# Masked attention layers: score products in fp32 on row strips, masks single-buffered; eight-bit feed-forward in stages

## What is computed

```python
x = x + attn(layernorm(x), ctx, ctx, mask...)     # layers 0, 1, 3
  q = (xn @ wq + bq), k = (ctx @ wk + bk), v = (ctx @ wv + bv)    # 16 heads of 16
  scores = q @ k.T / 4 (+ adj, layer 1);  masked -> NEG
  out = softmax(scores) @ v @ wo + bo
x = x + ffn_fp8(layernorm(x))                     # layer 2
  x_q = (bf16(xn) / s_in).astype(float8_e4m3fn);  k_q = (kernel / s_k).astype(float8_e4m3fn)
  y = bf16((x_q @ k_q) * (s_in * s_k)) + bias
```

## Time and profile before

| | us |
|---|---|
| median of three runs | 4533.09 |
| the profiled execution: its time / its span | 4538.09 / 4536.3 |
| TensorE / VectorE / ScalarE / GpSimd busy | 3469.7 / 2668.9 / 1727.2 / 1143.6 |
| mean granted TensorE clock | 0.868 of 2.4 GHz |
| attention 0 / 1 / 3 (stretches of the span) | 772 / 929 / 768 |
| fp8 feed-forward | 129 |
| bytes moved by DMA | 430 MB |

### The profile page before, as it was taken

How to read it: one execution, slowest core, us unless ns; L and a number is a source line. 1 busy time by engine, 2 the same in 40 slices (tenths; PEclk the granted TensorE clock), 3 DMA queues, 4 the chain that set the end, 5 groups by cost and what they waited for, 6 DMA issues and landing times. The chain is left out here.

```text
span 4536.3 us, 66863 instructions
## 1 busy us (share of the span) xinstructions
PE 3469.7 (76%) x17919; PEld 1709.7 (38%) x18053; DVE 2668.9 (59%) x7644; ACT 1727.2 (38%) x2466; POOL 1143.6 (25%) x1198
## 2 busy tenths in 40 slices
PE   2999998896477777867967777777325989997697
PEld 0343343443122222225634444444212334335465
DVE  1666665775488888974215555556664656663531
ACT  0454544442143344442115545555212545552011
POOL 3533430000643344201112222221004211201122
PEclk7999999898688888888988888888657999996699
DMA  5553550002544344310048888888224344323133
GB/s 123 96 101 67 99 90 16 5 1 58 109 110 85 85 85 89 67 44 0 0 82 238 225 223 229 224 234 239 68 50 64 55 69 67 55 36 103 34 97 74
DMA packets 198806, 430.47 MB, mean 95 GB/s; under 512 B 25392, under 2 KB 77456, under 8 KB 193696
## 3 DMA queue, kind: packets, MB, share of 16 engines
q1 hardware_dynamic: 192288, 417.74, 39.6%
q0 software_dynamic: 6144, 8.39, 1.1%
HBM read 265.38 MB, written 134.22 MB: 88 GB/s over the span
## 5 line engine op out<-in xcount | busy, mean ns | idle before, releaser
L420 DVE CUSTOM_DVE_ANT_0 A_sums<-A_p_ps,A_bias 128x512 bf16<-128x512 f32 x1536 | 1005.7, 686 | 560.7 <-PE A_p_ps L267 534.9
L493 ACT ACTIVATE A_probs<-A_p_ps 128x1024 f32<-128x1024 f32 x512 | 522.8, 1023 | 548.6 <-PE A_p_ps L285 546.9
L267 PE MATMUL A_p_ps<-A_k_stack,A_q_stack 96*128 96x512 bf16 x1536 | 537.8, 401 | 199.1 <-DVE A_nmax L420 191.1
L281 PE MATMUL A_p_ps<-A_q_stack,A_k_stack 99*128 99x512 bf16 x1536 | 477.3, 393 | 5.6 <-issue 2.4
L295 PE MATMUL A_oT_ps<-A_probs,A_v_aug 128*17 128x512 f32 x3072 | 435.2, 639 | 6.3 <-ACT A_probs L493 4.4
L493 ACT ACTIVATE A_probs<-A_probs 128x1024 f32<-128x1024 f32 x256 | 270.6, 1057 | 429.0 <-DVE A_probs L435 428.6
L267 PEld LDWEIGHTS A_p_ps<-A_k_stack,A_q_stack 96*128 96x128 bf16 x1536 | 138.9, 99 | 621.9 <-DVE A_nmax L420 529.1
L1070 DVE CUSTOM_DVE_ANT_0 A_scores<-A_qk_ps,A_rel_in 128x384 f32<-128x384 f32 (+3 forms) x512 | 232.1, 486 | 203.2 <-PE A_qk_ps L955 122.7
L978 PE MATMUL A_t_ps<-ident,A_scores 128*128 128x128 f32 x1280 | 226.2, 316 | 139.2 <-DVE A_probsT L1060 127.9
L435 DVE TENSOR_TENSOR A_probs<-A_p_ps,A_biasT 128x1024 f32<-128x1024 f32 x256 | 311.4, 1218 | 3.8 <-PE A_p_ps L281 3.4
L285 PE MATMUL A_p_ps<-A_biasT,ident_bf 128*128 128x512 bf16 x906 | 281.2, 380 | 7.2 <-issue 0.7
(11 more groups left out here) (341 smaller groups left out, 5407.4 us busy)
## 6 DMA issues: line engine op xcount, KB each, us to landing
A_parts_dram<-A_parts SPq DMA_DIRECT2D x48, 768.0 KB, 4.2
A_k_stack<-A_parts_dram SPq DMA_DIRECT2D x144, 256.0 KB, 9.8
A_q_stack<-A_parts_dram SPq DMA_DIRECT2D x144, 256.0 KB, 9.5
A_rel_dram<-A_rel_out SPq DMA_DIRECT2D x64, 512.0 KB, 4.4
A_rel_in<-A_rel_dram SPq DMA_DIRECT2D x64, 512.0 KB
A_rel_dram<-A_rel_out SPq DMA_DIRECT2D x64, 384.0 KB, 3.4
A_rel_in<-A_rel_dram SPq DMA_DIRECT2D x64, 384.0 KB, 4.1
A_ctxT<-in_ctxT SPq DMA_DIRECT2D x32, 512.0 KB, 12.4
```

The costliest lines, as they stand in the source:

```text
L267: nc.tensor.matmul(p1_ps[i % 2][:, :], q_stack[0:KS, a_par, j * GH + i, t * P:(t + 1) * P], k_stack[0:KS, a_par, j * GH + i, :], start=Tru ...
L281: last = nc.tensor.matmul(p2_ps[half][:, i % 2, :], k_stack[:, par, j * GH + i, kb * P:(kb + 1) * P], q_stack[:, par, j * GH + i, :], star ...
L420: nc.vector.tensor_tensor_reduce(out=sums[:, i % NX, :], in0=p1_ps[i % 2][:, :], in1=bias[:, (par + over) % NB, t, :], scale=-1.0, scalar= ...
L493: nc.scalar.activation(dst, src, ACT.Exp).then_inc(exp_done, 1)
```

## The change

In the three masked layers:

- q and k are stored once, in fp32, without parts: `q_stack` and `k_stack` become `[P, 2, NG, S]`, where head i of a group has rows 32i to 32i+15 (and 32i+16 is the row of maxima, against a row of ones in `k_stack`). Each product takes one strip of 32 rows. Splits, `parts_dram` and its stores go; a stack is loaded by 4 DMAs from `qk32` in SBUF (before: 1 store and 6 loads through DRAM). Maxima are turned in fp32 and placed by one DMA (before: 4).
- a position issues pass 1 and pass 2 by turns, on strips 0, 2, 1, 3 (p even) or 2, 0, 3, 1 (p odd), after all its waits.
- pass 1 and pass 2 each have a ring of three banks. ScalarE takes one head at a time (128x512).
- in layer 1 VectorE adds the bias to every other head (`LATE`); for the others TensorE adds it as three bf16 parts (`highT`, `midT`, `lowT`), three identity products.
- masks have one buffer, converted one block at a time, late in the frame; the hardware loop is written out; xT moves to 12 and 15, k to 18 and 20, and the first frame starts at p = 7.

`ffn_fp8`: ScalarE normalises, scales, multiplies for the overflow and copies the turned rows; VectorE keeps statistics, four of the rounding passes, the last add and the residual (one 128x1024 tile); buffers are doubled or tripled and the batches are staggered by one to three turns.

```diff
+    RW = P // GH
+    RING = 3
+    PAIRS = ((2, 3), (0, 1))
+    LOADS = GH
-        q_stack = sb("q_stack", [KS + 3, 2, H, S], BF16)
-        k_stack = sb("k_stack", [KS + 3, 2, H, S], BF16)
+        q_stack, k_stack = sb("q_stack", [P, 2, NG, S], F32), sb("k_stack", [P, 2, NG, S], F32)
-        p1_ps = [pb(f"p1_ps{i}", [P, S], F32) for i in range(2)]
-        p2_ps = [pb(f"p2_ps{i}", [P, 2, S], F32) for i in range(2)]
+        p1_ps = [pb(f"p1_ps{i}", [P, S], F32) for i in range(RING)]
+        p2_ps = [pb(f"p2_ps{i}", [P, S], F32) for i in range(RING)]
-        BY_DVE = (0, 1) if adj is not None else ()
+        LATE = (0, 2) if adj is not None else ()
+        TURNED_PARTS = (biasT,) if adj is None else (highT, midT, lowT)
-        FRONT = [(17, "k", 0), (20, "k", 1), (23, "xT", 0), (24, "xT", 1), (25, "q", 0), (28, "q", 1)]
+        FRONT = [(12, "xT", 0), (15, "xT", 1), (18, "k", 0), (20, "k", 1), (25, "q", 0), (28, "q", 1)]
-        START = 16
+        START = 7
+        def scores_read(n):
+            return (biased, adds(n + 1)) if by_dve(n) else (exp_done, n + 1)
...
+                    if later(unit + 2 - RING):
+                        pe.wait_ge(maxed, unit + 2 - RING)
+                    for k in (n, n + 1):
+                        if k >= RING:
+                            pe.wait_ge(*scores_read(k - RING))
+                for k in range(2):
+                    if first:
+                        i = 2 * half + k
+                        rows = slice(RW * i, RW * i + HD)
+                        nc.tensor.matmul(p1_ps[(unit + k) % RING][:, :], q_stack[rows, a_par, j, t * P:(t + 1) * P],
+                                         k_stack[rows, a_par, j, :], start=True, stop=True).then_inc(p1_done, 1)
+                    if second:
+                        i = PAIRS[half][k]
+                        rows = slice(RW * i, RW * i + HD + 1)
+                        last = nc.tensor.matmul(p2_ps[(n + k) % RING][:, :], k_stack[rows, par, g, kb * P:(kb + 1) * P],
+                                                q_stack[rows, par, g, :], start=True, stop=by_dve(n + k))
+                for k in range(2):
+                    if second and not by_dve(n + k):
+                        for part in TURNED_PARTS:
+                            last = nc.tensor.matmul(p2_ps[(n + k) % RING][:, :], ident_bf[:, :], part[:, kb, :],
+                                                    start=False, stop=part is TURNED_PARTS[-1])
+                        last.then_inc(p2_done, 1)
...
+            for i in range(GH):
+                sp.dma_start(stack[RW * i:RW * i + HD, par, :, :],
+                             qk32[i // 2:P:2, which, i % 2, :]).then_inc(stack_ready[which], 16)
...
@@ ffn_fp8
+            for n in range(B + 3):
+                if n + 1 < B:
+                    if n:
+                        statistics(n + 1)
+                    aggregate(n + 1)
+                if 0 <= n - 2 < B:
+                    finish_rows(n - 2)
+                if 0 <= n - 1 < B:
+                    round_rows(n - 1)
+                if 0 <= n - 3 < B:
+                    residual(n - 3)
...
+            for n in range(B + 2):
+                if n < B:
+                    normalise(n)
+                if n >= 2:
+                    turned(n - 2)
+                if 1 <= n <= B:
+                    overflow(n - 1)
+                if n >= 2:
+                    scaled_back(n - 2)
```

More of the change, by code:

```diff
@@ L188, in has @@
         def has(b, s):
[L190 removed]
+            return 0 <= b * STEPS + s < B * STEPS
         def ahead(s):
@@ L201, in group_split, with adds, by_dve @@
             return j if has(b, j * TPB) else None
-        def adds(step):
-            return step * len(BY_DVE)
+        def adds(n):
+            return n // GH * len(LATE) + sum(place < n % GH for place in LATE)
+        def by_dve(n):
+            return n % GH in LATE
+        def scores_read(n):
+            return (biased, adds(n + 1)) if by_dve(n) else (exp_done, n + 1)
         def pe_shared(pe, n, kind, i, base, b, par):
@@ new lines, in masked_attention, with mask_steps, pool_mask @@
+        MASK_STEPS = (lambda k: 1 + (k >= TPB)) if adj is not None else (lambda k: 0)
+        def mask_steps(bn, k):
+            return bn * sum(MASK_STEPS(i) for i in range(MK)) + sum(MASK_STEPS(i) for i in range(k))
+        def pool_mask(pool, bn, k):
+            done = (bn - 1) * STEPS + (NG - 1) * TPB + k % TPB + 1
+            if k < TPB and later(bn):
+                pool.wait_ge(maxed, done * GH)
+            if k >= TPB and later(bn):
+                pool.wait_ge(p2_done, done * GH)
+                if LATE:
+                    pool.wait_ge(biased, adds(done * GH))
+            dst = (bias if k < TPB else biasT)[:, k % TPB, :]
+            pool.wait_ge(mask_here[k % 2], (bn * (MK // 2) + k // 2 + 1) * MASK_LOADS)
@@ new lines, in pool_frame @@
+        def pool_frame(pool, b, par):
+            after, then = has(b, 0) and has(b + 1, 0), has(b + 2, 0)
+            for s in range(STEPS):
+                if s == 0 and every_mask and has(b, 0) and later(b):
+                    pool_mask(pool, b, MK - 1)
+                if s == 3 and has(b + 1, 0):
+                    pool_residual(pool, b + 1)
+                if s == 4 and then:
+                    pool_norm(pool, b + 2)
+                if s in (6, 7, 8, 9) and after and every_mask:
+                    pool_mask(pool, b + 1, s - 6)
+                if s in (13, 14, 15) and after and every_mask:
+                    pool_mask(pool, b + 1, TPB + s - 13)
@@ new lines, in overflow, with turned @@
+            def overflow(b):
+                act.wait_ge(rounded, b + 1)
+                if b >= 2:
+                    act.wait_ge(xq_ready, b - 1)
+                nc.scalar.activation(over[:, b % 2, :], v[:, b % 3, :], ACT.Copy, scale=FP8_PASS).then_inc(over_ready, 1)
+            def turned(b):
+                act.wait_ge(xqT_done, b + 1)
+                if b >= 2:
+                    act.wait_ge(y_done, (b - 1) * 2)
+                nc.scalar.activation(xqT[:, b % 2, :, :], t_ps[b % 2][:, :, :], ACT.Copy).then_inc(xqT_ready, 1)
```

621 lines of the change are left out of this document (268 added, 353 removed).

## The result

The changed kernel takes 4684.68 us (median of four runs, 4674.0 to 4690.51), the kernel before in the same rounds 4534.59 (4532.85 to 4550.21): a ratio of 1.032, 95% interval 1.0291 to 1.035. It is slower, by 150 us; 4662 was forecast. The profiled execution took 4686.68 us (span 4684.9), where the sum of the prediction came to 4667. One of the four executions of experiment 1 took 5313.95 us, at a mean granted clock of 0.63, and is left out of that experiment's median and ratio.

The account below looks back on a forecast made before the run. TensorE bounds layers 0 and 3, its loop with VectorE layer 1, VectorE the fp8 stage. On 4538.1 us: +70, +71, +30, -42 (layers 0, 3, 1, fp8) give 4667, median 4662; own range 4590 to 4760, full range 4450 to 4880.

Parts of the forecast that it names:

- (a): Score products, layers 0 and 3: four fp32 row strips run at once, 0.86 us a half, no change; upper bound 3.44.
- Partial overlap: Rival: strips overlap in part, 0.09 us paid for each of four strips, 207 us more, 4870 us; chance 0.16.
- no overlap: Rival: strips run one after another, 2.58 us a half, 1980 us more, 6640 us; chance 0.06.
- The rival of the clock: Rival: granted clock of layers 0 and 3 falls from 1.00 to 0.87, 175 us more, 4840 us; chance 0.04.
- (b): TensorE, layers 0 and 3: three more mode changes and unhidden first weights of two strip groups, 0.5 us a step, 8 a batch.
- The rival of free switches: Rival: strips next to full products cost nothing, 192 us less in the three masked layers, 4470 us; chance 0.27.
- (c): Ring of three banks, layers 0 and 3: uncovered even halves stall 0.73 us for exp, 5.4 us a batch.
- (d): Maxima, layers 0 and 3: m as four fp32 products costs 2.2 us a batch; 3 of 5.5 us of waits go.
- The last batch: Layers 0 and 3: half the halves lack pass 1, which saved 0.43 us each; strips last as long for two products, +6.
- Setup: Start of masked layers: first product at about 63 us, first frame 12 us longer; -30 layer 0, -29 layer 3, -15 layer 1.
- Layer 1: Loop between TensorE and VectorE of 2.75 us a half, plus about 5 us of delayed adds; batch 109 against 103, +45.
- fp8: Feed-forward stage: VectorE loses 48 us of work and waits, filling and draining the pipeline gives back 6; -42 us.

Follow-up runs that it names:

- experiment 1: The kernel before with only the new fp8 feed-forward, masked layers as they were; 4493.6 us, ratio 0.9895.
- experiment 5: The changed kernel with every group of four strips of layer 0 issued twice, the second overwriting the first with the same values; 4954 us.
- experiment 4: The changed kernel without mask products in layer 0 and with all score products of layer 3 reading the first strip of rows; 6053 us.
- Experiment 8: The changed kernel with one semaphore increment per group of value products instead of four, and in layer 0 one per two pass-1 products; 4668.77 us, ratio 1.0297.
- experiment 2: The changed kernel with four pieces of TensorE's shared work moved from odd halves to bare even halves; 4604.15 us, ratio 1.0142.
- experiment 3: The changed kernel, maxima over every fourth column in layers 0 and 3, two pass-1 and four pass-2 banks in layer 0; batches 90.0 us (layer 0), 93.8 (layer 3).
- experiment 6: The changed kernel with two banks for pass 1 and four for pass 2 in layer 0, maxima whole; 4720.9 us.
- experiment 7: The changed kernel with unused strips filled by products nobody reads, in the last batch of layers 0 and 3 and layer 0's first frame; 4650.74 us, ratio 1.0249.

## Why the prediction came out

**(a) The strips run at once: right.** Starts within 0.02 us, 0.86 us for a group without edges, 3.44 on one strip. Partial overlap and no overlap both fall. The rival of the clock falls for steady batches, which kept 1.00. The Trainium skill, "TensorE: Matmul & The Clock Gate", section "Measured speedup vs the span model", has 3.07 times for four row strips of 512 columns. Here a lone group of four fp32 products takes 1.07 us against 3.44, 3.2 times, and one that follows another 0.86, 4.0 times (experiment 5).

**(b) The switches: right, in both terms.** Three more changes at 0.11 us and 0.10 for each of the two strip groups make 0.53 us more for each step, where the prediction had 3 x 0.11 + 2 x 0.08 = 0.5. The rival of free switches falls with it. The Trainium skill, "TensorEngine Tiling (Array Packing)", section Tiling Modes, says that a change of mode drains the engine; the last pass ahead of each change is in fact 0.10 to 0.12 us longer, while two groups of one mode follow each other without a gap (experiment 5). The 0.10 at the start of a strip group is something else, since it is there without a change of mode too (experiment 4). That it is the load of the first weights, as the prediction says, is argued and not shown; the load (0.18 us) does begin together with the product, both at 546.58 in experiment 4. Experiment 8 excludes the increments.

**(c) The ring: right in mechanism and size.** 0.69 against 0.73 in bare even halves, 0.25 against 0.29 with a short turn, so 4.95 us a batch against 5.4; experiments 2, 3 and 6 show it from three sides. What was said to be queued behind the wait (pass 1 too) is what makes it dear.

**(d) The maxima: right, but the rest of VectorE's waits went too.** m costs 3.45 - 2.59 = 0.86 us a half (0.84 forecast). I kept 2.5 of the 5.5 us of waits for maxima in each batch; with three banks for pass 1, 0.2 us is left. Together with the 0.5 of the ring that is more than the 1.9 by which a batch came out lower than forecast (93.8 against 95.6; seven grew by 10.7 each, not 12.6). About 1 us goes the other way: a projection behind value products costs 1.92 us, not the 1.72 that I took.

**The last batch: the step that failed.** I gave it +12 us in all, and it took +36 in layer 0 and +32 in layer 3. Pass 1's absence saved 0.43 us a half before and saves nothing now, as I had written; but the clock, which I had priced only for the steady batches, falls there. Filled, and so at 1.00 to the end, the last batch takes 95.8 us: that is 12 us less in layer 3 and 16 in layer 0 (there in part the spread of executions), and still 20 more than before instead of 12. Waits for exp are 3 us of that (experiment 7's trace behind 804 us); the rest wasn't taken apart.

**Setup: nearly right.** The first product of pass 1 comes at 61.8 us (63 forecast). The first frame lasts 49 us where 42 was forecast, at a clock of 0.50 to 0.69. I had named the cold clock "at times"; it stayed for the whole frame, and the frame took 19 us more instead of 12. In layer 1 the first product came 24 us sooner and the first frame got 15 us longer: 9 us gained where 15 were forecast.

**Layer 1: one term too many.** The loop is as forecast: even halves 2.69 to 2.75 us (2.75), odd ones 2.81 (2.8). I added 5 us a batch for heads, norm and residual delaying an add; the sum without them is 103.9 us, and that is what a batch takes, not 109. One even half a batch lasts 3.40 us instead of 2.72; no more shows. The layer came out 12 us under the forecast, by this and in spite of its setup. The clock rose from 0.87 to 1.00 with TensorE busier.

**fp8: right, undersized.** 50 us instead of 42. VectorE's work fell by 34 us (105.7 to 71.6), near the 35 counted; its idle time fell by 16 (23.8 to 7.6), where 12.7 for the wait less 6 for filling and draining was counted.

**The sum.** 4687 against 4667: layer 0 +17, layer 3 +14, layer 2 +10 (its spread), layer 1 -13, fp8 -8. Terms of 41 us one way and 21 the other: that the sum is only 20 us off is luck in part.

## What to carry to other kernels

Products on strips cost where TensorE bounds the stage (layers 0 and 3). Layer 1 as changed was 17 us slower than before, and with the four moves 8 to 12 us faster; there half the adds also left VectorE, and that wasn't tried apart from the strips. Count every change between strips and whole array at 0.11 us and every group of row strips at 0.10 more, and lay products of one mode next to each other. When a ring of banks gets shorter, work out the loop product, exp, product for the half that has nothing else to do, and hang the loose work there: four moved pieces gave back half of what the change had cost. In stretches with few strips in use look at the granted clock, not only at the sum of products; filling free strips, or taking away the waits, can be cheaper than leaving them idle.

## What the runs showed of the hardware that I had not expected

- The granted clock can be low with TensorE busy for nine tenths of the time and more: 0.57 to 0.61 with all strip products on one strip (TensorE busy for 98%), 0.66 and 0.59 with two of four in use and a wait for exp in every bare even half, 1.00 in the same order with all four. With two in use and no such wait it was 1.00 too.
- Strips right behind strips cost nothing extra: eight fp32 products in two groups took 1.94 us, 1.72 of it their passes.
- Four increments on value products cost no more than one.
